# Second mixture: one operation per weight address, twelve result buffers, gathers that end 20 tiles early; slot tables of both mixtures with signs made on ScalarE

## What is computed

```python
# second mixture: 16 experts of width 192, 4 per row, and one shared expert
tidx, tw = _route(x, gate_w, gate_bias)
combine = zeros((n, E)).at[arange(n)[:, None], tidx].add(tw)
g = einsum('nh,eih->nei', x, w1); u = einsum('nh,eih->nei', x, w3)
y = einsum('nei,ehi->nh', silu(g) * u * combine[:, :, None], w2)
shared = (silu(x @ ws1.T) * (x @ ws3.T)) @ ws2.T
return y + shared
```

## Time and profile before

| | us |
|---|---|
| median of 3 runs (lowest, highest) | 1519.82 (1518.86, 1523.01) |
| the profiled execution | 1519.53 |
| its span in the trace | 1517.7 |
| first mixture, slot tables on DVE | 564.7 to 576.4 |
| second mixture, slot tables on DVE | 1208.6 to 1232.5 |
| second_tiles, first POOL gather to start of the last scatter | 1236.2 to 1466.1 |
| combine of the second mixture, first load to end | 1477.6 to 1515.5 |

### The profile page before, as it was taken

How to read it: one execution, slowest core, us unless ns; L and a number is a source line. 1 busy time by engine, 2 the same in 40 slices (tenths; PEclk the granted TensorE clock), 3 DMA queues, 4 the chain that set the end, 5 groups by cost and what they waited for, 6 DMA issues and landing times. The chain is left out here.

```text
span 1517.7 us, 41010 instructions
## 1 busy us (share of the span) xinstructions
PE 1192.2 (79%) x13450; PEld 869.1 (57%) x13450; DVE 1023.9 (67%) x2922; ACT 823.7 (54%) x2124; POOL 450.0 (30%) x480
## 2 busy tenths in 40 slices
PE   5899999998699528999999965966892165999950
PEld 2688888886345417988888842522572033766630
DVE  5699999997656777975544537333657976666636
ACT  6688888885588535854444413411646025666520
POOL 0555555552300000013333210200020037677740
PEclk9999999999899758999999965977995569999975
DMA  3433333332000274001111148298005312233328
GB/s 95 99 78 81 77 81 81 79 79 72 1 1 0 80 294 194 2 16 51 51 51 49 42 149 261 66 350 269 25 1 213 139 35 63 79 105 102 103 71 274
DMA packets 111807, 150.27 MB, mean 99 GB/s; under 512 B 13625, under 2 KB 96962, under 8 KB 111682
## 3 DMA queue, kind: packets, MB, share of 16 engines
q1 hardware_dynamic: 95730, 112.80, 23.8%
q0 software_dynamic: 11328, 30.95, 6.7%
q10 hardware_dynamic: 4624, 4.85, 1.0%
HBM read 126.80 MB, written 21.76 MB: 98 GB/s over the span
## 5 line engine op out<-in xcount | busy, mean ns | idle before, releaser
L1266 ACT ACTIVATE mixture_and_attentions_h<-ps,mixture_and_attentions_b 128x128 f32<-128x128 f32 x440 | 125.6, 373 | 126.2 <-PE ps L1218 124.9
L1218 PE MATMUL ps<-xture_and_attentions_m_w 128*128 128x128 f16 x1872 | 155.7, 219 | 1.8 <-DVE xture_and_attentions_m_w L1296 1.8
L1218 PEld LDWEIGHTS ps<-xture_and_attentions_m_w 128*128 x1872 | 129.1, 98 | 36.2 <-issue 2.6
L1540 POOL DMA_INDIRECT tage_second_mixture_rows<-n_rows,e_second_mixture_r_token x79 | 90.2, 1141 | 140.5 <-SPq L1371 116.7
L641 POOL TENSOR_TENSOR ads_and_recurrence_ctx_s<-ads_and_recurrence_ctx_c,ads_and_recurrence_ctx_s 128x512 f16<-128x512 f32 x64 | 74.2, 1160 | 177.6 <-ACT ads_and_recurrence_ctx_s L570 177.6
L1304 DVE TENSOR_SCALAR ixture_and_attentions_hs<-mixture_and_attentions_h 128x512 f16<-128x512 f32 x110 | 47.2, 429 | 112.7 <-PE ps L1237 97.6
L590 ACT ACTIVATE ads_and_recurrence_probs<-ps,s_and_recurrence_neg_max 128x257 f32<-128x257 f32 x256 | 117.7, 480 | 1.1 <-DVE s_and_recurrence_neg_max L672 1.1
L1236 PE MATMUL ps<-xture_and_attentions_m_w,ixture_and_attentions_hs 128*128 x312 | 117.5, 379 | 0.2 <-DVE xture_and_attentions_m_w L1315 0.2
L1335 POOL DMA_INDIRECT ture_and_attentions_rows<-n_rows,e_and_attentions_r_token x39 | 38.8, 994 | 261.2 <-SPq L1173 162.7
L1421 PE MATMUL ps<-stage_second_mixture_m_w,stage_second_mixture_x_s 128*128 x474 | 92.3, 332 | 2.1 <-issue 1.9
L1544 POOL DMA_INDIRECT y_rows<-stage_second_mixture_y,ge_second_mixture_r_dest x79 | 77.6, 982 | 39.4 <-issue 21.6
(11 more groups left out here) (395 smaller groups left out, 3325.4 us busy)
## 6 DMA issues: line engine op xcount, KB each, us to landing
ads_and_recurrence_ctx_t<-in_ctx_t SPq DMA_DIRECT2D x64, 257.0 KB, 2.7
e_and_attentions_b_ctx_t<-in_ctx_t SPq DMA_DIRECT2D x14, 1028.0 KB, 9.2
ure_and_attentions_b_ctx<-in_ctx SPq DMA_DIRECT2D x28, 512.0 KB, 7.8
xture_and_attentions_m_w<-in_m_w SPq DMA_DIRECT2D x2, 5632.0 KB, 37.3
ds_and_recurrence_mask_i<-in_mask SPq DMA_DIRECT2D x256, 32.1 KB, 1.7
stage_second_mixture_c_y<-y_rows SPq DMA_DIRECT2D x16, 512.0 KB, 4.9
stage_second_mixture_m_w<-in_m_w SPq DMA_DIRECT2D x2, 3840.0 KB, 20.5
xture_and_attentions_m_w<-in_m_w SPq DMA_DIRECT2D x1, 5120.0 KB, 16.6
```

Source lines behind the costliest of these rows:

```text
L1218: last = pe.matmul(ps[:, UB + 2 * (u % 2) + f // PER, (f % PER) * P:(f % PER + 1) * P], slots.of(e, c, at, P), a[:, c, :], start=(n == 0), ...
L1266: last = act.activation(h32[n][:, at:at + P], ps[:, UB + 2 * (u % 2) + n, at:at + P], ACT.Silu, scale=1 / (WS * NS), bias=b1[:, bass.ds(e ...
L1540: pool.indirect_dma_start(rows[s % R][:, :], None, k.n_rows, bass.IndirectOffsetOnAxis(ap=r.token[:, s:s + 1], axis=0)).then_inc(k.t_rows[ ...
```

## The change

- `weight` in second_tiles puts the high/low offset into the address before the register is used, so that the address needs one register operation and no second addition.
- Result buffers y: 12 instead of 4 (Y). A result tile waits for the scatter 12 tiles back.
- Row buffers: R = 48 in batches of six. Before scatter s, POOL has issued min(44 + 35 * (s + 1) // 59, 79) gathers: 44 ahead of the first scatter, the last one 20 tiles before the end.
- The high half of the 16 shared tiles is made by DVE (line 1505's operation), not by ACT.
- route: hot_hi is no longer made by DVE. ACT makes `side` by one Sign per pair over NTL + 1 columns, with hi_f (now -hi - 0.5) as per-partition bias; PE multiplies hot_lo by it; at the end ACT copies the bank out halved, and one DVE subtraction of neighbouring columns (held) gives what the bank held before. Eight buffers instead of four. PE waits for two semaphores per pair. A one-column Sign before the loop loads ACT's table. This holds for both mixtures.
- Some semaphores are shared by stages that do not overlap (x_rows, ctx_t_loaded).

```diff
+    NTS, AHEAD = NTL + 1, 8
@@ route, tensor
-                    pe.matmul(ps[:, SB, kk * NTL:(kk + 1) * NTL], hot_lo[u % 4][:, :], hot_hi[u % 4][:, :], start=(t == 0), stop=(t == NT - 1)).then_inc(k.m_placed.sem, 1)
+                    pe.wait_ge(k.m_side.sem, k.m_side.at(u + 1))
+                    pe.matmul(ps[:, SB, kk * NTS:(kk + 1) * NTS], hot_lo[u % AHEAD][:, :], side[u % AHEAD][:, :], start=(t == 0), stop=(t == NT - 1)).then_inc(k.m_placed.sem, 1)
@@ route, scalar
+            act.activation(warm[:, :], k.ident_h[:, 0:1], ACT.Sign)
+            act.wait_ge(k.m_ranked.sem, k.m_ranked.at(1))
+            for kk in range(K):
+                for t in range(NT):
+                    u = kk * NT + t
+                    act.wait_ge(k.m_placed.sem, k.m_placed.at(u - AHEAD + 1))
+                    act.activation(side[u % AHEAD][:, :], iota_h[:, 0:NTS], ACT.Sign, bias=hi_f[:, kk, t:t + 1]).then_inc(k.m_side.sem, 1)
+            act.wait_ge(k.m_placed.sem, k.m_placed.at(NT * K))
+            act.activation(halves[:, :, :].rearrange("p k n -> p (k n)"), ps[:, SB, 0:K * NTS], ACT.Copy, scale=0.5).then_inc(k.m_halved.sem, 1)
@@ route, vector
-                    dve.tensor_scalar(hot_hi[u % 4][:, :], iota_h[:, 0:NTL], hi_f[:, kk, t:t + 1], None, ALU.is_equal).then_inc(k.m_onehot.sem, 1)
+            dve.wait_ge(k.m_halved.sem, k.m_halved.at(1))
+            dve.tensor_tensor(held[:, :, :], halves[:, :, 1:NTS], halves[:, :, 0:NTL], ALU.subtract).then_inc(k.m_chain.sem, 1)
@@ second_tiles
-    R = 32
+    BATCH = 6
+    R, Y = 8 * BATCH, 12
-                both = slots.of(expert(u), 0, 2 * lo, 2 * n).rearrange("p (b x n) -> p b x n", x=2, n=P)
-                return both[:, :, x, :]
+                both = slots.of(expert(u), 0, 2 * lo + x * P, 2 * n).rearrange("p (b x n) -> p b x n", x=2, n=P)
+                return both[:, :, 0, :]
@@ scalar
-                if u + 3 < NT:
-                    high(u + 3)
@@ vector
                     multiply(u + 3)
-                    if u + 3 >= NT:
-                        high(u + 3)
+                    high(u + 3)
                     low(u + 3)
@@ gpsimd
-                while gathered < min(R - 4 + (mix.tiles - R + 4) * (s + 1) // (mix.tiles - 12), mix.tiles):
+                while gathered < min(R - 4 + (mix.tiles - R + 4) * (s + 1) // (mix.tiles - 20), mix.tiles):
```

More of the change, by code:

```diff
@@ L138, in _ @@
             dve.memset(k.eps[:, :], EPS / NS ** 2)
+    for g in range(G):
+        k.x_rows[g].base += 1
 def stage_weights(k, ctx, plain, split):
@@ L722, in _ @@
                 own(B // 2 - 1, 1)
+    for p in range(2):
+        k.ctx_t_loaded[p].base += B // 2
     return after_attention(k, o_t, k.w["L0_xattn_wout_t"])
@@ L1015, in route @@
         packed = k.sb("packed", [P, NTL], ctx=ctx)
-        hot_lo = [k.sb(f"hot_lo{p}", [P, P], F16, ctx=ctx) for p in range(4)]
-        hot_hi = [k.sb(f"hot_hi{p}", [P, NTL], F16, ctx=ctx) for p in range(4)]
+        hot_lo = [k.sb(f"hot_lo{p}", [P, P], F16, ctx=ctx) for p in range(AHEAD)]
+        side = [k.sb(f"side{p}", [P, NTS], F16, ctx=ctx) for p in range(AHEAD)]
+        warm = k.sb("warm", [P, 1], F16, ctx=ctx)
+        halves = k.sb("halves", [P, K, NTS], ctx=ctx)
+        held = k.sb("held", [P, K, NTL], ctx=ctx)
         iota_h = k.sb("iota_h", [P, P], F16, ctx=ctx)
@@ L1374, in second_tiles @@
         h_t = [k.sb(f"h_t{b}", [P, 3, P], F16, ctx=ctx) for b in range(3)]
-        y = [k.sb(f"y{b}", [P, D], ctx=ctx) for b in range(4)]
+        y = [k.sb(f"y{b}", [P, D], ctx=ctx) for b in range(Y)]
         rows = [k.sb(f"rows{b}", [P, 2 * D], F16, ctx=ctx) for b in range(R)]
@@ L1379, in loads @@
         def loads(batch):
-            return sum(min(4, mix.tiles - 4 * n) for n in range(batch % 8, batch + 1, 8))
+            return sum(min(BATCH, mix.tiles - BATCH * n) for n in range(batch % 8, batch + 1, 8))
         def source(u):
@@ L1481, in _ @@
                 silu(u)
-                high(u)
             flipped(0)
@@ L1518, in result @@
                     return
-                if s >= 4:
-                    dve.wait_ge(k.t_stored[s % 4].sem, k.t_stored[s % 4].at(s // 4))
-                dve.tensor_scalar(y[s % 4][:, :], out, 1 / (WS * HS), None, ALU.mult).then_inc(k.t_ycopied.sem, 1)
+                if s >= Y:
+                    dve.wait_ge(k.t_stored[s % Y].sem, k.t_stored[s % Y].at(s // Y))
+                dve.tensor_scalar(y[s % Y][:, :], out, 1 / (WS * HS), None, ALU.mult).then_inc(k.t_ycopied.sem, 1)
             for u in range(3):
                 multiply(u)
+                high(u)
                 low(u)
@@ L1551, in _ @@
                 scatter(s)
-            for b in range(4):
-                pool.wait_ge(k.t_stored[b].sem, k.t_stored[b].at((mix.tiles + 3 - b) // 4))
+            for b in range(Y):
+                pool.wait_ge(k.t_stored[b].sem, k.t_stored[b].at((mix.tiles + Y - 1 - b) // Y))
     for s in (k.t_up, k.t_act, k.t_gated, k.t_high, k.t_low, k.t_flip, k.t_hcopied, k.t_down, k.t_ycopied):
@@ L1557, in second_tiles @@
         s.base += mix.tiles
-    for b in range(4):
-        k.t_stored[b].base += (mix.tiles + 3 - b) // 4
+    for b in range(Y):
+        k.t_stored[b].base += (mix.tiles + Y - 1 - b) // Y
     for s in range(mix.tiles):
-        k.t_rows[s // 4 % 8].base += 1
+        k.t_rows[s // BATCH % 8].base += 1
     slots.finish()
@@ L2279, in build @@
         k.m_onehot = k.count("m_onehot", 2)
-        k.m_placed = k.count("m_placed", 4)
+        k.m_placed = k.count("m_placed", 8)
+        k.m_side = k.count("m_side")
+        k.m_ranked = k.count("m_ranked")
+        k.m_halved = k.count("m_halved")
         k.m_shift = k.count("m_shift")
@@ L2284, in build @@
         k.m_cwt = k.count("m_cwt")
-        k.t_trans = k.count("t_trans", 32)
+        k.t_trans = k.count("t_trans", 48)
         k.t_xcopied = k.count("t_xcopied", 2)
@@ L2337, in build @@
         k.t_rows = [k.count(f"t_rows{p}", unit=16) for p in range(8)]
-        k.t_stored = [k.count(f"t_stored{p}", unit=16) for p in range(4)]
-        k.x_loaded = [k.count(f"x_loaded{g}", unit=16) for g in range(G)]
+        k.t_stored = [k.count(f"t_stored{p}", unit=16) for p in range(12)]
         start(k)
```

52 lines of the change are left out of this document (23 added, 29 removed).

## The result

| | us | ratio to before |
|---|---|---|
| before, median (lowest to highest) | 1520.92 (1518.86 to 1523.01) | |
| after, median (lowest to highest) | 1483.73 (1483.49 to 1486.06) | 0.9759, 95% interval 0.9741 to 0.9777 |
| forecast | 1496.0 (1490.5 to 1503.5) | |

A forecast was written before the change was run, and what follows sets the result against it. POOL was taken to bound second_tiles and DVE route. Gains of 12.8 us in second_tiles and 10.8 in route sum to 23.6, and 1519.5 - 23.6 = 1495.9, forecast as 1496 us, range 1490.5 to 1503.5.

The forecast's parts named there:

- The holds of POOL: second_tiles, gathers before the first scatter: each meeting a DVE cast takes 2.17 us instead of 0.95; twelve casts add 14.6.
- term of 16.1 us: second_tiles, way to the first scatter: 14.6 us for twelve casts plus about 1.5 us for closer casts and copies.
- the sum of 217.1: POOL's time in second_tiles, first gather to last scatter, after the change: 214.5 + 1.6 + 1.0 us, gaining 12.8.
- the 214.5: second_tiles: POOL's 229.9 us from first gather to last scatter, less 15.4 us of idle time.
- the 1.0 for the copies: second_tiles: 16 high halves made by DVE while POOL gathers lengthen POOL's steps by 0.04 to 0.06 us each.
- High halves "in the sum: none": second_tiles, cast steps: period 3.73 falls to 2.7 to 2.9 us, some 10 us on PE's side, none counted.
- The rule on the port: DVE and POOL's shared port as an exclusive lock: 16 copies might each block POOL some 0.26 us, 4.2 in all.
- Addresses "costed at zero": second_tiles, PE's weight addresses: at most 0.1 us a tile, 8 us over 79, beside POOL's work, so zero.
- the rival "PE is the bound at the end": second_tiles: cast steps stay at 3.73 us, PE sets the end, gain 6.7 instead of 12.8, 1502 us; chance 0.18.
- No pause before the first scatter: second_tiles: POOL's 13.56 us standstill before its first scatter goes, 13.3 us of idle time removed.
- Slot tables: route: pairs at 0.25 us in the second mixture, 0.22 in the first; net gain 6.9 + 3.9 = 10.8 us.
- The slower rival: second_tiles: PE stops in small pieces, its clock falls to 1.2 GHz, kernel over 0.3% slower; chance 0.04.

The follow-up runs named there:

- the old order: Changed kernel with 28 gathers ahead of the first scatter, the last 12 tiles before the end, batches of four, twelve result buffers kept: 1497.21 us, ratio 0.9857.

## Why the prediction was wrong, step by step

**The holds of POOL: the step that failed.** The prediction says "a gather that meets a cast of 1.49 us takes 2.17 instead of 0.95, 1.22 more; twelve casts add 14.6", and adds that closer casts may hold longer, up to 1.49. It took one row of a pattern that repeats for the price of a meeting. The price depends on where in the cast the gather starts, and in before that was the worst place, 0.14 us inside, in ten meetings of eleven, because of the period. I had the numbers to see it: the new period of 2.7 to 2.9 stood two paragraphs below, and the two starts of the earlier trace rows gave 0.14 us. On the way to the first scatter the term of 16.1 us measured 3.6. In the sum of 217.1 it stands as the 13.1 us of holds that the 214.5 took over from before and 1.6 on top, 14.7: the 11.1 us between are most of the 12.8 missed, the 1.0 for the copies is another part, and 0.7 is not traced.

**High halves "in the sum: none".** The period was right (2.76, forecast 2.7 to 2.9), and so was DVE as its bound. The cost to POOL was not 1.0 but next to nothing: no gather that started outside a cast took over 0.99 us in after's first 44. In all traces together 85 gathers started inside such a copy of 128x192, and the longest took 1.07 us. And the worth was not slack for PE only: 10.4 us taken away from the change, 11.7 us in the block of before.

**The rule on the port.** The Trainium skill, "SBUF — State Buffer", section "SBUF: two separate sides", gives the port pair that DVE and GpSimd share to whichever starts first, a DVE operation in a two-port mode or with two inputs in SBUF (as this cast has) or a GpSimd operation, for its whole instruction, and has the other fully blocked. I left out "whichever starts first" and weighed the rule as a price for each cast and copy. Read in full it agrees with half of what the trace shows: a gather that starts inside a cast waits for its end, and the gather at 1242.80, which started first, went on for 0.79 us inside a cast without a delay. The other half is not seen here: the cast that started inside that gather took 1.48 us, and so did every one of 82 such casts in all traces (1.48 to 1.49). By the rule read as I did the copies would have cost 4.2 us.

**Addresses "costed at zero".** Right for before: alone they gave 1.3 us, which can't be told from nothing. My bound was 0.1 us a tile, 8 us; they took 0.22 us a tile off the results (2.08 to 1.86), beyond the bound, which looked at one gap and not at every sixth tile. They counted because the first step failed: with 16 us of holds PE would by the sum have had the slack that I gave it, but with 3.6 the old addresses make PE the bound and the block 9.1 us longer. So the rival "PE is the bound at the end" comes true once the gathers are faster, and it is the addresses that kept it away.

**No pause before the first scatter:** right. Worth 13.3 in the sum, 13.6 by the row of the old order, and 16.4 in the block, with PE's waits for gathers in it.

**The parts don't add up.** Taken away one at a time from the block they are worth 16.4, 10.4 and 9.1 us, 35.9 together, while all of them gave 25.6 of block: each that is missing lets another engine or the first result be the bound. Added alone to before, the addresses give nothing and the high halves 11.7.

**Slot tables:** right, 10.4 of 10.8 us. ACT's Sign sets the pace in the second mixture, (1221.0 - 1205.1) / 63 = 0.252 us (forecast 0.25), and the first has (573.24 - 566.32) / 31 = 0.223. Each Sign takes 344 ns. My estimate from the figures of the Trainium skill, "ScalarE: Activation LUTs", section "What ACT_TABLE_LOAD costs", was 0.254 for the pace, and the trace agrees. The tail was dearer than forecast; 0.2 us of it is the reduction, which now reads SBUF and not PSUM (0.68 us, before 0.47):

```profile
1221.75 0.44 ACT L1059 ACTIVATE ge_second_mixture_halves<-ps 128x320 f32<-128x320 f32 x1 [0.40 <-PE ps L1044]
1222.22 0.49 DVE L1141 TENSOR_TENSOR tage_second_mixture_held<-ge_second_mixture_halves 128x316 f32<-128x316 f32 x1 [2.16 <-ACT ge_second_mixture_halves L1059]
...
1223.15 0.68 DVE L1144 TENSOR_REDUCE age_second_mixture_row_f<-tage_second_mixture_held 128x79 f32<-128x316 f32 x1
```

**The slower rival:** no sign of it. With PE 20.00 of 20 us busy the granted clock is 1.00, its upper level of 2.4 GHz.

## What to carry to other kernels

When an operation is lengthened by another engine in a repeating pattern, don't carry its longest duration over as a price: read where it starts inside the other's, and work out the phase again with the new period. An edit that takes an engine off a loop's critical path changes that period, and so can be worth more on a third engine than on the two that it touches. A step costed at zero for lack of need is only zero while the bound beside it stands; work it out once more with that bound gone.

## What the runs showed of the hardware

A DMA issue on POOL that starts inside a DVE cast of 1.49 us waits and ends 0.82 us after it (0.95 us becomes 2.17, 1.20 or 1.13, by how much of the cast is left); one that starts 0.07 or 0.15 us ahead of the cast takes 0.94 or 0.95 as if alone, and so did two that started 0.01 and 0.04 us inside, while a third at 0.04 was held. The cast itself takes 1.48 to 1.49 us whether or not a gather is under way when it starts.

An added constant behind a register address on PE costs far more than the visible gap: 2.08 against 1.86 us a tile, with a tile of 2.5 to 2.7 us at every sixth. On the sequencer it showed as 241 fused register operations of 95 ns and 225 single ones of 35 in 100 us, against 61 of 61 ns and 463 of 33.

The same kernel can run at two levels, 1520 and 1600 us for before. At the slower one PE, ACT and DVE stand still for some 45 us while POOL issues gathers, and ACT starts up to 26 us after the end of the PE products that it waits for (0.04 us in most tiles of the changed kernel at the faster one); the cause was not found.
